# Filler matmuls left out of two attention pipelines, outside the fill of each

## The reference, cut to what matters

```
x = _layernorm(x + _L0_attn_ref(x, ...))          # first token: full attention; the others: window of +-16
x = _layernorm(x + _L0_xattn_ref(x, ctx_512, ...)) # causal self attention plus cross attention to ctx
x = _layernorm(x + _L0_ffn_ref(x, ...))            # 16 experts, each takes its top 64 tokens
x = _layernorm(x + _L1_attn_ref(x, ...))           # gated recurrence and a gated MLP
x = _layernorm(x + _L1_xattn_ref(x, ctx_512, ctx_512, ...)) # cross attention
x = _layernorm(x + _L1_ffn_ref(x, ...))            # 8 experts, top 2
```

## Time and profile before

| | us |
|---|---|
| median of 3 runs | 703.16 |
| lowest, highest | 701.92, 704.52 |
| the profiled execution, its own time | 705.27 |
| its span, first to last instruction | 703.5 |
| PE busy / DVE / ACT / POOL | 535.8 / 380.8 / 217.9 / 137.9 |
| mean granted TensorE clock | 0.86 of 2.4 GHz |

### The profile page before, as it was taken

The page is one execution under the profiler, slowest core; times in us unless marked ns, Lnnn a source line. Parts: engine busy times, 40 slices in busy tenths (PEclk is TensorE's granted clock), DMA queues, the critical chain, the costliest instruction groups (busy, mean ns, idle before and its releaser), DMA issues. The chain is left out here.

```text
span 703.5 us, 10323 instructions
## 1 busy us (share of the span) xinstructions
PE 535.8 (76%) x3940; PEld 311.5 (44%) x3940; DVE 380.8 (54%) x799; ACT 217.9 (31%) x441; POOL 137.9 (20%) x174
## 2 busy tenths in 40 slices
PE   4629999989999997211899835776399998679994
PEld 2406765655656563100378712353134554323331
DVE  1366554675666771479834455345566752344464
ACT  2101554446455665010111004212015566022121
POOL 4282302422132300520000010006412100300000
PEclk9568999999999999555889987695559989789998
DMA  9311211111111100510000030000201100000000
GB/s 323 155 43 52 60 32 47 48 47 47 47 48 47 47 3 0 210 63 0 1 1 1 2 135 0 0 1 0 76 15 47 47 2 1 2 0 0 1 15 15
DMA packets 32401, 29.56 MB, mean 42 GB/s; under 512 B 2912, under 2 KB 31072, under 8 KB 31840
## 3 DMA queue, kind: packets, MB, share of 16 engines
q1 hardware_dynamic: 32352, 28.90, 13.2%
HBM read 15.52 MB, written 0.52 MB: 23 GB/s over the span
## 5 line engine op out<-in xcount | busy, mean ns | idle before, releaser
L804 DVE TENSOR_REDUCE nmax<-bank 128x2 f32<-128x512 f32 (+2 forms) x240 | 142.1, 624 | 105.3 <-PE bank L610 54.5
L722 ACT ACTIVATE arena<-bank 128x512 f32<-128x512 f32 (+2 forms) x256 | 128.3, 525 | 119.4 <-PE bank L631 48.0
L610 PE MATMUL bank<-arena 66*128 66x256 bf16 (+2 forms) x512 | 92.5, 270 | 29.6 <-DMA arena<-qkl 26.4
L383 PE MATMUL bank<-causal_qk,identb 128*128 128x512 bf16 x266 | 91.9, 442 | 13.1 <-PEq L844 8.6
L631 PE MATMUL bank<-arena 68*128 68x256 bf16 (+2 forms) x512 | 86.9, 257 | 8.7 <-ACT arena L722 6.0
L610 PEld LDWEIGHTS bank<-arena 66*128 66x128 bf16 x512 | 46.2, 102 | 60.0 <-DMA arena<-qkl 27.9
L662 PE MATMUL bank<-arena 128*32 128x256 f32 (+4 forms) x1088 | 60.9, 345 | 2.1 <-ACT arena L722 1.9
L631 PEld LDWEIGHTS bank<-arena 68*128 68x128 bf16 x512 | 46.0, 98 | 32.7 <-ACT arena L722 16.2
L383 PEld LDWEIGHTS bank<-causal_qk,identb 128*128 128x128 bf16 x266 | 27.6, 110 | 47.2 <-issue 28.1
L662 PEld LDWEIGHTS bank<-arena 128*32 128x32 f32 x1088 | 27.3, 110 | 23.6 <-issue 9.0
L1499 DVE TENSOR_TENSOR arena<-bank,arena 128x512 f32<-128x512 f32 x24 | 16.6, 691 | 32.0 <-ACT arena L1454 32.0
(11 more groups left out here) (274 smaller groups left out, 858.9 us busy)
## 6 DMA issues: line engine op xcount, KB each, us to landing
arena<-qkl SPq DMA_DIRECT2D x192, 64.0 KB
fcw<-in_fc1T SPq DMA_DIRECT2D x1, 4096.0 KB, 17.5
arena<-in_fc2T SPq DMA_DIRECT2D x1, 4096.0 KB, 14.7
fcw<-in_last SPq DMA_DIRECT2D x1, 2304.0 KB, 8.2
w<-in_w SPq DMA_DIRECT2D x1, 1216.0 KB, 6.2
rows<-in_rows SPq DMA_DIRECT2D x1, 704.0 KB, 7.6
xT<-in_xT SPq DMA_DIRECT2D x1, 512.0 KB, 3.6
x<-in_x SPq DMA_DIRECT2D x1, 512.0 KB
```

The costliest lines, as they stand in the source:

```text
L383: nc.tensor.matmul(bank[:, :], m.identb[:, :], m.causal_qk[:, 0:4, :], start=True, stop=True)
L610: ins = t.matmul(out[:, i, :], m.qstack[n % 3][0:66, h, qt * P:(qt + 1) * P], m.kstack[n % 3][0:66, h, k0:k1], start=(i == 0), stop=(j.kin ...
L722: s.activation(m.prob[h % 8][:, 0:w], ST[c % NST][:, 0:w], ACT.Exp).then_inc(exps, 1)
L804: v.tensor_reduce(m.nmax[n % 2][:, qt, h0:h0 + nh], MX[c % NMX][:, 0:nh * (k1 - k0)].rearrange("p (h k) -> p h k", h=nh), AX.X, ALU.max, n ...
```

## The change

It takes out `keep_warm` at four of the six places in `attention_pipeline`, for every job:

```
-F_STACK, F_FILL, F_SHIFT, F_OTT, F_YT = 3, 1, 3, 1, 2
+F_FILL = 1
...
                 n = at(slot, S_OTT)
                 if n is not None:
                     pe.wait_ge(m0_read, m0_no["ott", n])
-                    keep_warm(nc, m, M0, F_OTT)
                     pe.wait_ge(ot_in, n + 1)
...
                     pe.wait_ge(m0_read, m0_no["yt", n])
-                    keep_warm(nc, m, M0, F_YT)
                     pe.wait_ge(y_ready, n + 1)
...
-                        keep_warm(nc, m, MX[c % NMX], 2 * WARM if n == 0 else F_STACK)
+                        if n == 0:
+                            keep_warm(nc, m, MX[c % NMX], 2 * WARM)
                         pe.wait_ge(stack[n % 3], 192 * (n // 3 + 1))
...
                     if h == 0:
-                        keep_warm(nc, m, ST[c % NST], F_SHIFT)
                         pe.wait_ge(shift[n % 3], 32 * (n // 3 + 1))
```

## The result

| | before | after |
|---|---|---|
| median, us | 703.84 (4 runs) | 729.63 (4 runs) |
| lowest, highest | 701.92, 705.52 | 719.12, 733.04 |
| the profiled execution, own time | 705.27 | 733.04 |
| its span | 703.5 | 731.3 |
| mean granted TensorE clock | 0.86 | 0.783 |

The change makes the kernel slower: by the medians 3.7%, and the ratio of after to before is 1.0274 with a 95% interval of 1.0167 to 1.0381. The ratios in this document leave out executions over 1.5% longer than the fastest of their kernel, here the two longest of four; since that spread is part of the effect, as will be seen, the medians of all executions stand beside them. The shortest execution of the changed kernel, 719.12 us, is still 13.6 us above the longest of before. The forecast was 690.5 us, in a range of 684 to 703.

The account below looks back on a forecast made before the run. The prediction took PE to bound both pipelines. Fillers removed give 17.7 us, less 5 us for further clock falls, 12.7 us net: 703.16 - 12.7 = 690.5 us, in a range of 684 to 703.

Parts of the forecast that it names:

- What bounds the kernel: Both attention pipelines: PE is busiest, 204.73 of 224 us in layer 0 and 87.29 of 95 us in layer 1.
- The gain group by group: Both layers: removing 130 fillers gains 12.5 us in layer 0 and 5.2 in layer 1, 17.7 us together.
- six of the twelve groups: Layer 0, fillers ahead of the maxima: six groups pay in full, 6 x 0.65 = 3.9 us.
- four singles: Layer 0: four of 12 single fillers have idle for `ot` behind them and give 0; eight give 0.22 us each.
- The stack waits: Layer 0: new PE waits for stack DMAs at three jobs, 1.0, 0.3 and 0.2 us, take 1.5 us of the gain.
- What it costs, the clock: Both pipelines: without fillers PE drops to 1.2 GHz more often, costing 5 us, between 0 and seven more falls possible.
- two more such falls: In the two pipelines: two further drops to 1.2 GHz at 2.5 us each on average, 5 us in all.
- the one rise without a filler: Layer 0, 174.9 to 178.3 us: the clock came back without a filler, so falls there were expected to be short.
- its twin at 212.87: Layer 0: same 1.15 us idle as near 174.9, but three fillers shortly ahead at 209.05; clock stayed at 1.00.
- Layer 1 stays at 1.2 GHz: Rival, second pipeline: own matmuls fail to restore the clock over two jobs, 35 x 0.8 = 28 us lost, 713 us; chance 0.10.
- The page's rule on short idles: Trainium skill rule cited for a rival: short idles between matmul groups while PSUM banks are cycled move the clock up and down.
- What would show it: Signs: 136 fillers left, layer 0 some 10 us and layer 1 some 3 us shorter; wrong if second-pipeline clock well under 0.84.

Follow-up runs that it names:

- g1_rows: The change, with score matmuls contracting over 126 and 128 rows instead of 66 and 68, the added rows zeros on q's side; 683.78 us.
- g3_rows_before: The kernel before with all its fillers, plus score matmuls contracting over 126 and 128 rows in place of 66 and 68; 695.39 us.
- e2_l1_out: The kernel before with the four kinds of fillers left out in layer 1 only (33 of 130); 720.96 us, ratio 1.022.
- f4_burst: The change plus two bursts of 12 fillers in layer 1, ahead of the heads of jobs 0 and 2; 712.69 us, ratio 0.9993.
- e4_thin: The kernel before with the 130 fillers kept in place at 512 columns but narrowed to 32 rows and 32 columns of the array; 749.78 us.
- e3_long_warm: The change with 72 (layer 0) and 62 (layer 1) warm-up fillers instead of 16 ahead of the first stack wait; 706.05 us, 692.14 to 724.76.

## Why the prediction was wrong, by its own steps

**What bounds the kernel: right.** PE bounds both pipelines. `g1_rows` against `g3_rows_before`, which differ only in the 130 fillers at a clock that holds, are 683.78 and 695.39 us: leaving the fillers out is worth 11.6 us.

**The gain group by group: right in kind, too large.** I had 17.7 us, within bounds of 12 and 28.6; the 11.6 us lie just below the lower one. In the profiles of `g3_rows_before` and `g1_rows`, from the start of the first max unit to the start of the last two x of each pipeline, layer 0 takes 230.1 and 220.4 us, a gain of 9.8 where I had 12.5, and layer 1 takes 88.5 and 86.2 us, a gain of 2.4 where I had 5.2. The spacing of 0.22 us stands (0.13, by the Trainium skill's "TensorE: Matmul & The Clock Gate", section "Back-to-back issue gap", would have made the sum 10.6; that this is nearer is chance, since the spacing in the traces is 0.22 throughout). What was too small is what the waits take. PE waits in the pipeline of layer 0 of `g1_rows` (60 to 266 us):

```profile
PE bank L631 <- DMA arena<-nmT: 5.4, 8, 1.4
PE bank L582 <- ACT ot L714: 4.0, 5, 1.5
PE bank L610 <- DVE nmax L804: 1.7, 3, 0.6
PE bank L610 <- DMA arena<-qkl: 1.4, 2, 1.1
```

With the fillers, in `g3_rows_before` (60 to 275 us), the first two were 1.4 us at 3 places and 1.7 us at 3. The maxima's DMA is waited for at 8 places: I had counted six of the twelve groups as paying in full, because no idle stood behind their fillers, without asking how much slack the DMA had. The wait for `ot` more than doubled, where I had only four singles, 0.9 us, lost in it. The stack waits came about as worked out (1.4 us at 2 places, where I had 1.5 us new at 3; the longest 1.1 for 1.0). Which wait took the rest in layer 1 was not followed up.

**What it costs, the clock: the step that failed.** "At half clock a PE-bound stretch does half its work, so the two falls cost 1.7 and 3.4 us" priced a fall by the lengths it had with the fillers in, and the sum had two more such falls, 5 us. What came instead are stretches of 41.0 and 47.8 us at 0.50, and a fill of layer 1 that stayed low until 554 us. In layer 1 the fillers were what had ended such stretches: without them it stayed low but for 3.4 us (`e2_l1_out`), and each burst of 12 lifted it (`f4_burst`). I took the one rise without a filler, at 178.3 us, as the rule for layer 0; it stands right behind a projection (L565 at 177.09), and after the change the projections at 152.77 and 162.61 us did not bring the clock back, so that the stretch lasted 41.0 us.

The price in the terms of the sum: `g1_rows` is the changed program at a clock that holds, so the clock took 729.63 - 683.78 = 45.9 us of the change. Of the kernel before it took 10.3 us already (`g3_rows_before` against 705.71). What the change adds is 35.5 us, or 37.4 if it is taken as the loss of 25.8 us plus the 11.6 us that the fillers were worth (the kernel before read 1.9 us higher beside `g1_rows` than beside the change). The sum had 5 in its place.

A reading behind this step was wrong too. I told the fall at 174.9 from its twin at 212.87 by the three fillers ahead of the twin. The fall has the same three, at the same distance:

```profile
170.95 0.81 PE L383 MATMUL bank<-causal_qk,identb 128*128 128x512 bf16 x3
```

From there to the matmul behind the idle are 3.82 us, as from 209.05 to 212.87, with the same matmuls between. So these rows do not say why one place fell and the other did not.

**The rival that came.** "Layer 1 stays at 1.2 GHz" had its place, its mechanism and its evidence right, at a chance of 0.10 and 713 us. It had its price per microsecond too high: with 85.8 us at 0.50, layer 1 is in the profile 28.5 us longer than in `g1_rows` (first L609 at 515.5 to the last x at 630.4, against 492.2 to 578.7), a third of the stretch, that is 0.5 for each microsecond of full-clock steps where I had 0.8. Its length was too short: I counted two jobs of layer 1, and it was most of layer 1 and a part of layer 0. With the evidence of the fill, PE busy 17.67 of 18 us at 0.50, it deserved a far larger chance.

**The page's rule on short idles.** The falls come behind idles of about 1 us (1.18 and 0.84 us ahead of the stretch of 41.0). The Trainium skill has short idles as a cause in "TensorE: Matmul & The Clock Gate", section "A second HAM failure mode: psum-queue depth-cycling"; that agrees. But the loss is not, as that section has it, paid in going up and down between bursts: PE went down seldom and stayed. The same page says, under "What's actually happening", that activity releases the throttle. With PE busy 47.36 of 47.8 us it was not released, so the busy time of the profile does not tell it here; `e4_thin` and `g1_rows` differ from their counterparts in the part of the array that matmuls use, and the clock went with that.

**What would show it.** Fillers that remain are 136 in the program (124 of them have matmul records in the trace). The granted clock of the second pipeline, named as the sign of the last rival, was 0.52 over 505 to 600 us, where it had been 0.84.

## What to carry to other kernels

Ask of a filler what ends a low stretch without it, before you price its time: look in the trace for a stretch at 1.2 GHz in which PE is busy throughout. If there is one, the kernel's own matmuls there do not bring the clock back, and any fall may be long. Before paying for fillers, try work in the array that costs no time; here it was a contraction over zero rows up to 126 and 128.

## What the runs showed of the hardware that was not expected

- Busy time alone did not bring the clock up: 0.50 for 47.8 us with PE busy 47.36 us, again in a second kernel to the tenth of a microsecond (47.38 of 47.8).
- Rows of zeros count. With 126 and 128 rows in place of 66 and 68 in the two score matmuls, nearly half of them zeros against ones, the pipelines hold 0.99 at the same number of matmuls, and the kernel goes from 729.63 to 683.78 us. Fillers of 32 x 32 with the same 512 columns gave 749.78 us.
- The same idle with the same matmuls and fillers ahead of it fell once and held once (174.9 and 212.87 us before).
- Where the clock sometimes holds, the executions spread: 14 us for the change, 33 us with `e3_long_warm`, against 4 to 9 us for the kernel before in its four sets of runs and 5 us for `g1_rows`.
- Not tried: whether the rows would do in one of the two kinds of score matmul alone, and how few they may be. Not shown: why one projection raised the clock and another did not.
